# Merging eight task matrices in two row groups of the array, with the up and down products set between the merges

## What is computed

```python
# hidden size F = 1024, H = 256, E = 8 tasks; gate: [16, 8], one row per sequence b
W1_b = W1 + sum_e gate[b, e] * TW1[e]      # [F, H]
W2_b = W2 + sum_e gate[b, e] * TW2[e]      # [H, F]
hidden = gelu(x_b @ W1_b.T + b1_b)         # [64, F]
x_b    = x_b + hidden @ W2_b.T + b2_b
```

## Time and profile before

| | us |
|---|---|
| median of 3 runs | 2373.8 (2371.68 to 2376.3) |
| the profiled execution | 2377.73 |
| its span, first to last instruction | 2375.9 |
| the feed-forward part, from the first load to the last statistics | 1344 to 1578.5 of the span |
| TensorE busy over the span | 2179.1 (92%) |
| VectorE busy over the span | 1314.4 (55%) |

### The profile page before, as it was taken

One profiled execution on the slowest core, in us unless ns is written; L12 is line 12 of the kernel. 1 busy time (PEld: TensorE's weight loads), 2 busy tenths in 40 slices (PEclk: granted clock), 3 DMA queues, 4 the chain that ended last, 5 costly groups with the idle time before them and its releaser, 6 DMA issues. The chain is left out here.

```text
span 2375.9 us, 39783 instructions
## 1 busy us (share of the span) xinstructions
PE 2179.1 (92%) x15922; PEld 1507.1 (63%) x15922; DVE 1314.4 (55%) x2266; ACT 994.0 (42%) x1858; POOL 332.1 (14%) x366
## 2 busy tenths in 40 slices
PE   7999999999999977999998799978999998877796
PEld 4777777777777754555564677844555554545695
DVE  4556556656665634555553344347777772656554
ACT  1555555555555551343332011114666663515121
POOL 3322222222222200000000000032000000000231
PEclk9999999999999978999999899988999999898798
DMA  6877776777777521000000221123112111023312
GB/s 202 197 167 182 178 168 150 171 176 167 183 179 169 127 58 50 6 12 6 6 1 1 114 86 74 54 48 74 32 28 35 31 17 39 2 55 133 134 48 78
DMA packets 100570, 216.18 MB, mean 91 GB/s; under 512 B 58482, under 2 KB 66043, under 8 KB 94660
## 3 DMA queue, kind: packets, MB, share of 16 engines
q1 hardware_dynamic: 97652, 204.93, 34.9%
q0 software_dynamic: 2208, 6.03, 0.8%
q10 hardware_dynamic: 528, 2.69, 0.4%
HBM read 91.16 MB, written 15.20 MB: 45 GB/s over the span
## 5 line engine op out<-in xcount | busy, mean ns | idle before, releaser
L908 DVE TENSOR_REDUCE L_xattn_maxima<-L_xattn_scores 128x1 f32<-128x1024 f32 (+1 forms) x256 | 253.5, 990 | 249.2 <-PE L_xattn_scores L831 248.8
L975 ACT ACTIVATE L_xattn_probs_t<-L_xattn_turned 128x1024 f32<-128x1024 f32 (+1 forms) x256 | 220.8, 862 | 342.3 <-PE L_xattn_turned L843 342.3
L1812 DVE TENSOR_REDUCE shared_half_maxima<-shared_ring 128x1 f32<-128x578 f32 (+1 forms) x251 | 244.3, 990 | 88.3 <-PE shared_ring L1718 85.2
L1892 ACT ACTIVATE shared_exps<-shared_scores 128x512 f32<-128x512 f32 (+1 forms) x416 | 225.7, 594 | 122.5 <-PE shared_scores L1739 121.8
L987 ACT ACTIVATE L_xattn_probs<-L_xattn_scores,L_xattn_maxima 128x1024 f32<-128x1024 f32 (+1 forms) x256 | 235.6, 925 | 37.9 <-DVE L_xattn_maxima L911 37.9
L843 PEld LDWEIGHTS L_xattn_turned<-ident,L_xattn_probs 128*128 128x128 f32 x1664 | 198.0, 144 | 81.0 <-issue 48.1
L843 PE MATMUL L_xattn_turned<-ident,L_xattn_probs 128*128 128x128 f32 x1664 | 234.7, 281 | 14.1 <-ACT L_xattn_probs_t L975 12.0
L505 PE MATMUL L_xattn_projected<-L_xattn_wv,L_xattn_ctx 128*128 128x256 f32 x780 | 193.6, 390 | 0.0
L499 PE MATMUL L_xattn_projected<-L_xattn_ctx,L_xattn_wk 128*128 128x400 f32 x480 | 181.9, 501 | 0.0
L831 PE MATMUL L_xattn_scores<-L_xattn_k_stack,L_xattn_q_stack 128*128 128x512 f32 (+1 forms) x512 | 159.5, 393 | 22.2 <-ACT L_xattn_probs L987 11.1
L1739 PE MATMUL shared_scores<-shared_q,shared_k 128*128 128x512 f32 (+1 forms) x416 | 154.4, 449 | 0.1
(11 more groups left out here) (390 smaller groups left out, 3163.3 us busy)
## 6 DMA issues: line engine op xcount, KB each, us to landing
L_xattn_k_stack<-L_xattn_k_part SPq DMA_DIRECT2D x504, 200.2 KB, 4.3
L_xattn_ctx<-in_ctx_t SPq DMA_DIRECT2D x16, 1602.0 KB, 6.9
ffn_task<-in_ffn_task SPq DMA_DIRECT2D x16, 1024.0 KB, 6.7
experts_w_in<-in_expert_in SPq DMA_DIRECT2D x8, 1024.0 KB, 12.0
shared_k<-k_scratch SPq DMA_DIRECT2D x64, 100.1 KB, 3.3
L_xattn_q_stack<-q_scratch SPq DMA_DIRECT2D x128, 32.0 KB, 2.0
k_scratch<-L_xattn_shared_part SPq DMA_DIRECT2D x128, 32.0 KB, 1.7
shared_q<-q_scratch SPq DMA_DIRECT2D x64, 64.0 KB, 3.6
```

The source lines that it names most:

```text
L908: nc.vector.reduce_max(maxima[n % 2][:, half:half + 1], cols, axis=AX).then_inc(halves_maxed, 1)
L975: nc.scalar.activation(probs_t[:, t:t + m, p * P:(p + 1) * P], turned_tiles[:, 0:m, :], ACT.Copy).then_inc(turned_moved, 1)
L1812: nc.vector.reduce_max(half_maxima[:, n, half:half + 1], found[:, 0:HALF_STARTS[half + 1] - HALF_STARTS[half]], axis=AX).then_inc(ring_max ...
L1892: nc.scalar.activation(exps[n % 2][0:m, h * BANK:(h + 1) * BANK], scores[0:m, h, :], ACT.Exp, scale=SCALE).then_inc(exps_done, 1)
```

## The change

A merging product of 128 rows is split into two of 64 rows (`ROW_GROUPS`), one on rows 0 to 63 of the array and one on rows 64 to 127. Each covers 8 of the 16 features, so `spread` has 128 columns and not 256. Row group r writes bank r of `merging`. A unit is now four blocks (`MERGE_BLOCKS`), so eight products that fill both banks, and a tile has four units for each matrix. As a unit takes both banks, it may start only when the unit directly before it has been moved. VectorE moves 1024 elements for each partition at once. The up products are issued by sequence; a unit of merging stands before every second sequence, and the down products of the tile before follow the up products with a lag of two sequences. The waits of a tile stand now at its first sequence or at the first of a half.

```diff
-MERGE_UNITS = 8
+MERGE_BLOCKS = 4
+MERGE_UNITS = 16 // MERGE_BLOCKS
+ROW_GROUPS = 2
+GROUP_ROWS = P // ROW_GROUPS
+GROUP_SPREAD = SPREAD // ROW_GROUPS
...
-        spread = sb("spread", [P, BATCH, SPREAD])
+        spread = sb("spread", [P, BATCH, GROUP_SPREAD])
...
+        STEP_BATCHES = BATCH // (2 * MERGE_UNITS)
+        DOWN_LAG = 2
...
-                    if n >= 2:
-                        pe.wait_ge(merge_moved, n - 1)
+                    if n >= 1:
+                        pe.wait_ge(merge_moved, n)
                     for i, block_of in enumerate(blocks):
-                        last = nc.tensor.matmul(merging[:, n % 2, i * 2 * P:(i + 1) * 2 * P], block_of,
-                                                spread[:].rearrange("p b f -> p (b f)"), start=True, stop=True)
+                        for r in range(ROW_GROUPS):
+                            group = slice(r * GROUP_ROWS, (r + 1) * GROUP_ROWS)
+                            last = nc.tensor.matmul(merging[:, r, i * P:(i + 1) * P], block_of(group),
+                                                    spread[group].rearrange("p b f -> p (b f)"), start=True, stop=True)
                     last.then_inc(merge_done, 1)
...
+                def down(k, b):
+                    half, i = divmod(b, BATCH // HALVES)
+                    if b == 0:
+                        pe.wait_ge(merge_moved, second_units(k) + MERGE_UNITS)
+                    if i == 0:
+                        pe.wait_ge(hidden_ready, HALVES * k + half + 1)
+                    t, j = divmod(b, 2)
+                    last = nc.tensor.matmul(down_psum[j * SEQ:(j + 1) * SEQ, t // 2, (t % 2) * DIM:(t % 2 + 1) * DIM],
+                                            hidden_t[:, k, b * SEQ:(b + 1) * SEQ], merged_2[k % 2][:, b, :],
+                                            start=False, stop=k == HIDDEN_TILES - 1, skip_group_check=True)
...
-                merge_first(0)
+                for j in range(MERGE_UNITS):
+                    merge_first(0, j)
...
                 for m in range(HIDDEN_TILES):
-                    if m < HIDDEN_TILES - 1:
-                        merge_first(m + 1)
-                    up(m)
-                    merge_second(m)
-                    if m > 0:
-                        down(m - 1)
-                down(HIDDEN_TILES - 1)
+                    merges = [(merge_first, m + 1, j) for j in range(MERGE_UNITS)] if m < HIDDEN_TILES - 1 else []
+                    merges += [(merge_second, m, j) for j in range(MERGE_UNITS)]
+                    downs_done = 0
+                    for b in range(BATCH):
+                        if b % STEP_BATCHES == 0 and b // STEP_BATCHES < len(merges):
+                            merge, tile, j = merges[b // STEP_BATCHES]
+                            merge(tile, j)
+                        up(m, b)
+                        if m > 0:
+                            downs_due = max(b + 1 - DOWN_LAG, 0) * BATCH // (BATCH - DOWN_LAG)
+                            for i in range(downs_done, downs_due):
+                                down(m - 1, i)
+                            downs_done = downs_due
+                for b in range(BATCH):
+                    down(HIDDEN_TILES - 1, b)
```

More of the change, by code:

```diff
@@ L1382, in merge_unit @@
                     last.then_inc(merge_done, 1)
[L1384 to L1393, removed]
@@ L1395, in up @@
-                def up(m):
-                    pe.wait_ge(merge_moved, first_units(m) + MERGE_UNITS)
-                    for half in range(HALVES):
-                        if m > 0:
[L1399 to L1404, removed]
-                        last.then_inc(up_done, 1)
@@ L1407, in down, with merge_first @@
[L1407 to L1418, removed]
+                def merge_first(m, j):
+                    if j == 0:
+                        pe.wait_ge(task_1_loaded[m % 2], 16 * (m // 2 + 1))
+                    c, q = divmod(j, MERGE_UNITS // 2)
+                    merge_unit(first_units(m) + j, [lambda group, i=i: task_1[m % 2][group, c, MERGE_BLOCKS * q + i, :] for i in range(MERGE_BLOCKS)])
@@ new lines, in merge_second, with up @@
+                def merge_second(k, j):
+                    if j == 0:
+                        pe.wait_ge(task_2_loaded[k % 2], 16 * (k // 2 + 1))
+                    merge_unit(second_units(k) + j, [lambda group, i=i: task_2[k % 2][group, MERGE_BLOCKS * j + i, :] for i in range(MERGE_BLOCKS)])
+                def up(m, b):
+                    half, i = divmod(b, BATCH // HALVES)
+                    if b == 0:
+                        pe.wait_ge(merge_moved, first_units(m) + MERGE_UNITS)
+                    if m > 0 and i == 0:
+                        pe.wait_ge(hidden_ready, HALVES * (m - 1) + half + 1)
+                    for c in range(CHUNKS):
+                        last = nc.tensor.matmul(up_psum[:, half, i * SEQ:(i + 1) * SEQ], merged_1[m % 2][:, c, b, :],
+                                                xn_t[:, c, b * SEQ:(b + 1) * SEQ], start=c == 0, stop=c == CHUNKS - 1)
+                    if i == BATCH // HALVES - 1:
+                        last.then_inc(up_done, 1)
@@ new lines, in down @@
+                def down(k, b):
+                    half, i = divmod(b, BATCH // HALVES)
+                    if b == 0:
+                        pe.wait_ge(merge_moved, second_units(k) + MERGE_UNITS)
[5 more added lines that the diff above has]
+                                            start=False, stop=k == HIDDEN_TILES - 1, skip_group_check=True)
+                    if k == HIDDEN_TILES - 1 and b % 4 == 3:
+                        last.then_inc(down_ready, 1)
+                    if k < HIDDEN_TILES - 1 and b == BATCH - 1:
@@ L1440, in _, with merged_unit @@
                 for m in range(HIDDEN_TILES):
-                    if m < HIDDEN_TILES - 1:
-                        merge_first(m + 1)
-                    up(m)
-                    merge_second(m)
-                    if m > 0:
-                        down(m - 1)
-                down(HIDDEN_TILES - 1)
+                    merges = [(merge_first, m + 1, j) for j in range(MERGE_UNITS)] if m < HIDDEN_TILES - 1 else []
[13 more added lines that the diff above has]
+                    down(HIDDEN_TILES - 1, b)
             @block.vector
             def _(dve):
+                def merged_unit():
+                    return merging[:].rearrange("p r (i b f) -> p i r b f", b=BATCH, f=GROUP_SPREAD)
                 def move_first(m):
@@ L1457, in move_first @@
                         dve.wait_ge(merge_done, n + 1)
-                        f = 2 * SPREAD * q
+                        f = MERGE_BLOCKS * SPREAD * q
                         nc.vector.tensor_tensor(
[L1460 to L1463, removed]
+                            merged_1[m % 2][:, c, :, f:f + MERGE_BLOCKS * SPREAD].rearrange("p b (i r f) -> p i r b f", r=ROW_GROUPS, f=GROUP_SPREAD),
+                            merged_unit(),
+                            base_1[:, c, m * P + f:m * P + f + MERGE_BLOCKS * SPREAD].rearrange("p (i r f) -> p i r f", r=ROW_GROUPS, f=GROUP_SPREAD)
+                            .unsqueeze(3).to_broadcast([P, MERGE_BLOCKS, ROW_GROUPS, BATCH, GROUP_SPREAD]), ALU.add).then_inc(merge_moved, 1)
                 def move_second(k):
@@ L1470, in move_second @@
                         dve.wait_ge(merge_done, n + 1)
-                        d = 2 * SPREAD * j
+                        d = MERGE_BLOCKS * SPREAD * j
                         nc.vector.tensor_tensor(
[L1473 to L1476, removed]
+                            merged_2[k % 2][:, :, d:d + MERGE_BLOCKS * SPREAD].rearrange("p b (i r f) -> p i r b f", r=ROW_GROUPS, f=GROUP_SPREAD),
+                            merged_unit(),
+                            base_2[:, k, d:d + MERGE_BLOCKS * SPREAD].rearrange("p (i r f) -> p i r f", r=ROW_GROUPS, f=GROUP_SPREAD)
+                            .unsqueeze(3).to_broadcast([P, MERGE_BLOCKS, ROW_GROUPS, BATCH, GROUP_SPREAD]), ALU.add).then_inc(merge_moved, 1)
                 nc.vector.memset(gates[:], 1.0)
@@ L1486, in _ @@
                 nc.vector.scalar_tensor_tensor(
-                    spread[:], merging[:, 0, 0:BATCH].unsqueeze(2).to_broadcast([P, BATCH, SPREAD]), gb2_wide[:],
-                    spread_mask[:].unsqueeze(1).to_broadcast([P, BATCH, SPREAD]), ALU.add, ALU.mult).then_inc(spread_ready, 1)
+                    spread[:], merging[:, 0, 0:BATCH].unsqueeze(2).to_broadcast([P, BATCH, GROUP_SPREAD]), gb2_wide[:],
+                    spread_mask[:].unsqueeze(1).to_broadcast([P, BATCH, GROUP_SPREAD]), ALU.add, ALU.mult).then_inc(spread_ready, 1)
                 dve.wait_ge(gate_rows_ready, 1)
@@ L2792, in layouts @@
     d["gate_b2_wide"] = np.tile(i["L0_ffn_gate_b2"], SPREAD)[:, None]
-    d["spread_mask"] = (rows[:, None] // TASKS == np.arange(SPREAD)).astype(np.float32)
+    d["spread_mask"] = (rows[:, None] // TASKS % GROUP_SPREAD == np.arange(GROUP_SPREAD)).astype(np.float32)
```

2 lines of the change are left out of this document (1 added, 1 removed).

## The result

The changed kernel takes 2397.38 us (median of 4 runs, 2393.85 to 2404.37); beside it the kernel before took 2375.01 (4 runs, 2371.68 to 2376.3). The ratio is 1.0107 (95% interval 1.009 to 1.0123): slower by 1.1%. The prediction of 2371.9 is 25 us too low, and 2397 lies outside its range. The profiled execution took 2396.05 us (span 2394.2, granted clock 0.938 against 0.952 before).

The account below looks back on a forecast made before the run. TensorE alone was taken to bound the kernel. Entry 0.65, first tile -3.3, six tiles -2.0 and last tile +2.8 made -1.9 us, 2375.9 profiled and 2371.9 forecast; own range 2367 to 2377, with rivals 2362 to 2381.

Parts of the forecast that it names:

- with 1.6 for that again: First tile: 19.5 us warm plus 1.6 for the half clock makes 21.1, against 24.4 before: -3.3.
- the entry's 0.65: merge_first(0) before the loop: moves and units in series, first unit at 1.2 GHz, end about 1368.0 instead of 1367.36: +0.65 us.
- Rival 3: Tiles: the clock falls when less than the whole array is used; a quarter of their time at 1.2 GHz gives 2391; 10%.
- the forecast's signs of being wrong: A unit taking 1.8 us, up following merging without a gap, or the clock leaving 1.00 after 1380.
- the lone up pair: Tiles: four up records standing alone between other shapes take 0.53 us on TensorE, 14 of them a tile.
- The first tile's last slot: End of the first tile (m = 0): 2.1 us, after seven slots of 2.49, 19.5 warm in all.
- the two ups with the open wait: Behind a tile's first unit: two ups (0.98 and the 0.094) leave 0.41 of a 1.48 us wait for VectorE's move uncovered.
- the -1.9: Whole kernel: predicted change in us, summed from entry 0.65, first tile -3.3, six tiles -2.0 and last tile +2.8.
- Rival 1: Merging units: the row groups do not overlap, a unit takes 2.0 us, +57.6, so 2429; 8%.
- Rival 2: Up behind merging units: going between 64x128 and 128x128 is free, -6 to -9 us, 2363 to 2366; 13%.
- Rival 4: Tiles: single downs run beside their neighbours, -18 us, 2354; 3%.
- Rival 5: 14 bare waits and 250 changes of shape: longer moves or slower hand-overs, +20 ns each is +5, 2377; 4%.

Follow-up runs that it names:

- experiment 2: Changed kernel's order with unsplit merging products of 128 rows and 256 columns (ROW_GROUPS = 1); 2425.52 us, 1.0221 of the kernel before.
- Experiment 1: Changed kernel plus twelve thrown-away whole-array products of 512 columns right before the first tile; 2391.67 us (one run).
- experiment 6: Changed kernel with bias rows moved behind the first unit and five thrown-away whole-array products in the waits before the first tile; 2374.89 us, 1.0008 of the kernel before.
- experiment 7: Changed kernel, entry unchanged, with downs issued in pairs: a unit, two ups, two downs; 2367.39 us, 0.9988 of the kernel before.
- experiment 4: Changed kernel with each half-row merging product issued twice, same result; 2438.55 us (one run).
- experiment 5: Changed kernel with the eight 9-row bias products moved from behind the fourth unit to behind the first; 2391.43 us, 1.0091 of the kernel before.
- experiment 3: Changed kernel's split units put back in the order of the kernel before (all units, ups, units, downs); 2491.61 us, 1.0497 of the kernel before.

## Why the prediction was wrong

**The step that failed** is the first tile's "with 1.6 for that again", and with it the entry's 0.65. Both took over the clock's course from the kernel before, where 2.4 GHz came back about 1377, under a block of whole-array merging. The change replaced this very block by short units with ups between them, and the clock stayed at 1.2 GHz for about 82 us (from 1337.0 to 1419.0). With whole-array units in the same order (experiment 2) it was back 3.3 us into the first tile. The second tile, which the prediction counted as warm, was hit as well. This is 22.2 of the 28.5 us. Experiment 1 shows it from one side (raised beforehand, the clock stays and the tiles are 20.09 and 26.51), experiment 6 from the other (raised in the waits at no cost, the kernel is at 2374.89).

**Rival 3 named the clock, but the wrong event.** It asked whether the clock would *fall* in the tiles, and saw the single downs as the danger; it was given 10%. In the warm tiles it never fell (1.00 over 132.6 us). What was missing is the question whether it would *rise*, and the first tile, without any downs, was the place. The argument against rival 3 (the up blocks kept 1.00) was right for holding and says nothing for rising. Its 2391 comes near the result in size only, not by its mechanism. Of the forecast's signs of being wrong it was the clock's that showed, 0.50 after 1380.

**A term mis-sized**: the lone up pair, put at 0.53 us, measured 0.59 (1437.66 to 1438.25). The prediction took the same 0.094 for every change of shape. After ups, whose records have 64 columns, the next shape starts 0.15 beyond the columns. That is 14 x 0.06 = 0.84 a tile: 25.7 + 0.84 is the 26.5 measured, and 5.9 us over seven tiles. The first tile's last slot was put at 2.1, without the wait for VectorE's move ahead of the next tile's unit, and takes 2.58 warm (1403.21 to 1405.79 in experiment 1): most of the 0.6 there. 22.2 + 5.9 + 0.6 = 28.7 is the whole miss, to 0.2. The rows of before had no change of shape behind such short records, except that from up to merging, where none is paid.

**What held.** The unit (1.10 predicted, 1.09 measured), the single down and the pair (0.58; 0.58 and 0.59), the two ups with the open wait (1.48, 1.47), VectorE's move (1.22, 1.225), the last tile but for the ups (2.8 + 0.84 = 3.64, measured 3.7). Of the chances, the sum for slower adds up to 21% and not 22, which changes nothing here. That experiment 6 ends level with the kernel before (1.0008) does not bear out the -1.9, since its moved bias rows save 5.2 us that were no part of the forecast. Experiment 1 less its 12.1 us of extra products lies 6.9 us over the kernel before (one run), 4.0 of it the cold entry. By the forecast's own course of the clock, its -1.9 and the 6.5 mis-sized make about +4.6, an estimate.

**The other rivals.** Rival 1 (row groups in series) is out: pairs are 0.112 apart. The Trainium skill ("TensorEngine Tiling (Array Packing)", Key Properties) says that different tiles can load weights and multiply at the same time; the trace agrees, with 1.09 us a unit where a series, as the prediction worked out, would make it 2.0. Rival 2 (free change between 64x128 and 128x128) is out too: a unit's last columns end 0.90 after its first start, and the up comes at 1.09. The same section says that a change of tiling mode drains TensorE; the trace agrees, at 0.094 to 0.15 us and the uncovered load behind it. Rival 4 (single downs beside their neighbours) is out by 0.58. Rival 5, given 4%, is half right: the moves are not longer (1.225), but slower hand-overs at changes of shape are the 5.9 us above, close to its +5.

**Where the expected gain went.** The splitting is worth 5.3 us a tile when warm (experiment 2). The order that it needs cost 5.8 us a tile, for the single downs and the changes of shape, and this was priced rightly but for 0.84. So a warm tile is 0.5 us dearer than before, and the last one 3.7, against 4.5 saved in a warm first tile (24.58 to 20.09). Even with the clock up the change is slightly slower, and the clock at the entry made a small loss a large one. Pairing the downs takes 4.6 us a tile off (experiment 7), the fillers and the moved bias rows some 22 us once (experiment 6), and only with both is the change a gain.

**What stays open** is why this mix does not raise the clock. The half-row shape (experiment 4) and the 9-row products just ahead (experiment 5) were tried and are not it. Nor can it be only the changes of shape and the waits, since 13.6 us of up products without either stayed at 0.50 (experiment 3). In every kernel with the change's units and an unwarmed entry it stayed down through the first tile and rose in the second, where the down products come in; doubled units, whole-row units and fillers raised it sooner. That is what stood beside the rise; no run took the kinds of product apart, one at a time.

## What to carry to other kernels

Read the granted clock at the entry of a stage, and ask what raises it there: if a change thins out the dense block that stands behind a wait, price the whole stage at half speed as its own case, and look for waits in which a few thrown-away whole-array products can stand for nothing. When products are split or reordered to use parts of the array together, count the changes of shape and the neighbours that lose each other; keep one kind together in even numbers before judging the idea.

## What the runs showed of the hardware

- The clock has memory. The same tile of the same instructions took 31.25 us at 0.50 and 20.08 at 1.00, by what had run ahead of it, and each state lasted: 0.50 over the 31.25 us of the first tile, 1.00 for the rest of the part.
- A change of shape costs about 0.094 us beyond the columns behind records of 128 or 256 columns, and 0.15 behind records of 64.
- Work without a gap does not always raise the clock: 13.6 us of whole-array up products ran at 0.50 throughout (experiment 3).
- The clock can fall under waits that one engine's move sets: with 1.3 to 1.4 us of idleness between units it was at 0.50 for 34 of 41 us of each tile from the third on (experiment 3), a larger loss than the idleness: 28.05 busy us at half speed are 14 lost, the idle time beside them 6.
- 16 more half-row records in a unit took 0.99 us and not 0.90 (experiment 4); no cause was looked for.
